# Second attention of a two-layer block: value products in two column halves with their sums from a block of ones, absorbed queries in pairs of heads, the row of maxima carried by transfers

## What is computed

```python
q_hk  = (hidden_q @ Wq.T).reshape(Bv, Sv, H, K)            # H = 16, K = 128
q_big = apply_rope(einsum('bshk,hkq->bshq', q_hk, w_kc_q))  # 192 columns per head
kv_r  = apply_rope(kv_c)                                    # 1444 x 64
q_r   = einsum('bshq,hqr->bhsr', q_big, W_qr)
k_r   = einsum('bld,hdr->bhlr', kv_r, W_kr)
scores = einsum('bhsr,bhlr->bhsl', q_r, k_r)
attn  = softmax(scores, axis=-1)
ctx_c = einsum('bhsl,bld->bhsd', attn, kv_r)                # values are kv_r itself
ctx_lat = einsum('bhsd,hkd->bhsk', ctx_c, w_kc_kv)
out   = ctx_lat.reshape(...) @ Wo.T
```

## Time and profile before

| | |
|---|---|
| median of 3 runs | 3939.77 us |
| the profiled execution: its time, its span | 3932.55 us, 3930.8 us |
| PE busy | 3538.9 us, 90% of the span |
| DVE, ACT, POOL busy | 2027.9, 1375.3, 814.5 us |
| granted TensorE clock, mean | 0.94 of full |
| second attention, first wide product to last scores | about 945 to 3634 us |
| value products (L1352) | 3072 records, 1156.9 us |
| score products (L1340, L1341) | 3072 records, 630.5 and 538.3 us |

### The profile page before, as it was taken

How to read it: one execution, slowest core, us unless ns; L and a number is a source line. 1 busy time by engine, 2 the same in 40 slices (tenths; PEclk the granted TensorE clock), 3 DMA queues, 4 the chain that set the end, 5 groups by cost and what they waited for, 6 DMA issues and landing times. The chain is left out here.

```text
span 3930.8 us, 51787 instructions
## 1 busy us (share of the span) xinstructions
PE 3538.9 (90%) x16584; PEld 2434.5 (62%) x16592; DVE 2027.9 (52%) x3166; ACT 1375.3 (35%) x2778; POOL 814.5 (21%) x678
## 2 busy tenths in 40 slices
PE   6999799996999999999999999999999999999244
PEld 5777688884666566656656665665665666566122
DVE  5777644444543644544364454445445444542588
ACT  1333222221334243234324323433432343334256
POOL 0000122222210410311131131122014012210367
PEclk9999799997999999999999999999999999999666
DMA  3000100003000000000000000000000000000200
GB/s 94 0 0 0 41 0 0 0 11 86 7 18 15 9 17 17 13 8 19 17 5 17 18 12 14 15 17 3 17 19 11 15 13 19 3 16 9 76 11 23
DMA packets 65315, 69.40 MB, mean 18 GB/s; under 512 B 23464, under 2 KB 55560, under 8 KB 65026
## 3 DMA queue, kind: packets, MB, share of 16 engines
q1 hardware_dynamic: 65090, 66.55, 6.1%
HBM read 56.30 MB, written 10.04 MB: 17 GB/s over the span
## 5 line engine op out<-in xcount | busy, mean ns | idle before, releaser
L1352 PE MATMUL c_o_ps<-c_p,c_val 120*65 120x400 f32 (+1 forms) x3072 | 1156.9, 499 | 2.0 <-ACT c_onum L1198 2.0
L1084 DVE TENSOR_REDUCE c_mneg<-c_m_ps 128x1 fp32r<-128x1452 f32 (+1 forms) x448 | 746.7, 1667 | 748.7 <-PE c_m_ps L1263 748.0
L1221 ACT ACTIVATE c_p<-c_s_ps 120x400 f32<-120x400 f32 (+1 forms) x1536 | 691.2, 501 | 1041.2 <-PE c_s_ps L1341 1033.2
L1340 PE MATMUL c_s_ps<-c_q,c_k 128*120 128x400 f32 (+1 forms) x1536 | 630.5, 410 | 30.4 <-issue 28.1
L1352 PEld LDWEIGHTS c_o_ps<-c_p,c_val 120*65 120x65 f32 (+1 forms) x3072 | 420.6, 137 | 354.2 <-issue 315.6
L1341 PE MATMUL c_s_ps<-c_q,c_k 65*120 65x400 f32 (+1 forms) x1536 | 538.3, 350 | 0.0
L1263 PE MATMUL c_m_ps<-c_k,c_q 128*128 128x484 f32 (+1 forms) x1344 | 456.3, 448 | 19.0 <-DVE c_mneg L1084 9.8
L1263 PEld LDWEIGHTS c_m_ps<-c_k,c_q 128*128 128x128 f32 (+1 forms) x1344 | 231.0, 181 | 223.9 <-DVE c_mneg L1084 113.4
L1028 POOL TENSOR_TENSOR c_rot<-c_rc,c_rs 96x400 f32<-96x400 f32 x256 | 262.1, 1044 | 508.0 <-DVE c_rs L1113 265.1
L1340 PEld LDWEIGHTS c_s_ps<-c_q,c_k 128*120 128x120 f32 (+1 forms) x1536 | 285.7, 186 | 103.3 <-issue 76.5
L1341 PEld LDWEIGHTS c_s_ps<-c_q,c_k 65*120 65x120 f32 (+1 forms) x1536 | 286.9, 187 | 56.6 <-issue 39.1
(11 more groups left out here) (220 smaller groups left out, 4273.0 us busy)
## 6 DMA issues: line engine op xcount, KB each, us to landing
c_rdb<-l_denominators SPq DMA_DIRECT2D x64, 200.0 KB, 3.3
c_kv<-in_ctx SPq DMA_DIRECT2D x32, 360.0 KB
x_rows<-in_x SPq DMA_DIRECT2D x4, 800.0 KB
x_spill<-x_rows SPq DMA_DIRECT2D x1, 3200.0 KB
c_xa<-x_spill SPq DMA_DIRECT2D x8, 400.0 KB
c_xr<-x_spill SPq DMA_DIRECT2D x32, 100.0 KB
x_spill<-c_xr SPq DMA_DIRECT2D x32, 100.0 KB
d_rows<-x_spill SPq DMA_DIRECT2D x5, 640.0 KB, 11.3
```

Of the source, the lines that this page charges most:

```text
L1084: v.tensor_reduce(mneg[0:n, t, DL:DL + 1], m_ps[0:n, :, 0:4 * KP], AX.XY, ALU.max, negate=True).then_inc(mneg_ready, 1)
L1221: a.activation(p[0:k, u % 3, i * CQS // 2:(i + 1) * CQS // 2], s_ps[0:k, (2 * u + i) % 3, 0:CQS // 2], ACT.Exp).then_inc(exp_ready, 1)
L1340: pe.matmul(o, k1[j % 2][:, r * KP:r * KP + k], q1[:, j, cols], start=True, stop=False)
L1352: mm = pe.matmul(o_ps[0:VW, i, 0:CQS // 2], val[0:k, j % 2, r, :], p[0:k, u % 3, i * CQS // 2:(i + 1) * CQS // 2], start=(r == 0), stop=(r ...
```

## The change

1. **Values.** The 64 value rows are multiplied by the left and the right 400 columns into the two partition halves of one bank, `o_ps[i * 64 : (i + 1) * 64]`. The sums leave that product: a 120 x 32 block of ones is multiplied by four quarters of 200 columns, into partitions 0, 32, 64 and 96 of a bank `d_ps` of its own.
2. **Drain, normalisation.** One copy of 128 x 400 and one of 128 x 200 in place of two of 65 x 400; four short transfers spread the sums, two bring them back, and one multiplication of 128 x 400 takes the place of one of 64 x 800. The halves in `ct` are heads 0 to 3 and 4 to 7 of a chunk, so the order in which `cvo` is built changes too.
3. **Absorbed queries.** Two heads at a time, into the two partition halves of `d_ps`; the ring `rot` has four places; four copies and two subtractions follow per pair.
4. **Row of maxima.** `maxima_row` and its copy are gone. SP carries each of the seven columns `mneg[0:128, c, t]` to a stretch of row 64 of `q2`; the first scores of a chunk wait for all seven (`row_loaded`).
5. **Places.** In a group's head the keys are turned beside head 1 (was 3), the projection stands at head 5 (was 6), the maxima beside heads 4, 6, 7, 9, 10, 11, 12 (were 9 to 15); the projection beside tiles moves from tile 8 to 9. SP's order is rewritten.

```diff
-                        for i in range(2):
-                            mm = pe.matmul(o_ps[0:VW, i, 0:CQS // 2], val[0:k, j % 2, r, :], p[0:k, u % 3, i * CQS // 2:(i + 1) * CQS // 2],
+                        for i in range(2):
+                            pe.matmul(o_ps[i * DL:(i + 1) * DL, 0:HALFQ], val[0:k, j % 2, r, :], p[0:k, u % 3, i * HALFQ:(i + 1) * HALFQ],
+                                      start=(r == 0), stop=(r == NT - 1))
+                        for q in range(4):
+                            mm = pe.matmul(d_ps[q * 32:(q + 1) * 32, 0:QUART], ones[0:k, :], p[0:k, u % 3, q * QUART:(q + 1) * QUART],
                                            start=(r == 0), stop=(r == NT - 1))
...
+                def load_row(ch, j, c):
+
+                    sp.wait_ge(mneg_ready, PRIMED + (ch + 1) * NQT)
+                    sp.sem_inc(m.carrier, 1)
+                    for t in range(NQT):
+                        sp.dma_start(q2[DL:DL + 1, j, c * CQS + t * 128:c * CQS + t * 128 + QT[t]].bitcast(F32), mneg[0:QT[t], c, t:t + 1].bitcast(F32)).then_inc(row_loaded, 16)
...
                         if r == 0:
-                            pe.wait_ge(row_copied, PRIMED + (it * G + j) * CH + c + 1)
+                            pe.wait_ge(row_loaded, 16 * NQT * ((it * G + j) * CH + c + 1))
...
-                    sp.dma_start(den[:], onum[DL:DL + 1, :].rearrange("o (p f) -> o p f", p=S)).then_inc(den_loaded, 16)
+                    for i in range(4):
+                        sp.dma_start(den[i * S // 4:(i + 1) * S // 4, :], oden[32 * i:32 * i + 1, :].rearrange("o (p f) -> o p f", p=S // 4)).then_inc(den_loaded, 16)
...
-                    for i in range(2):
-                        a.activation(onum[:, i * CQS // 2:(i + 1) * CQS // 2], o_ps[0:DL + 1, i, 0:CQS // 2], ACT.Copy).then_inc(on_ready, 1)
+                    a.activation(onum[:], o_ps[:, 0:HALFQ], ACT.Copy).then_inc(on_ready, 1)
+                    a.activation(oden[:], d_ps[:, 0:QUART], ACT.Copy).then_inc(on_ready, 1)
...
+                    def absorbed(pair):
+                        n = gi * (H // 2) + pair
+                        pe.wait_ge(rot_ready, PRIMED + 4 * (n + 1))
+                        if pair >= 1:
+                            pe.wait_ge(q1_ready, PRIMED + 4 * n)
+                            pe.wait_ge(q2_ready, PRIMED + 2 * n)
...
+                        for a in range(2):
+                            for half in range(2):
+                                i = 2 * pair + half
+                                mm = pe.matmul(d_ps[half * DL:(half + 1) * DL, 0:T], m.mqk[:, a, HEADS[i], :], rot[:, i % 4, a, :], start=(a == 0), stop=(a == 1))
...
+        HEAD_MAX, HEAD_PROJECT = (4, 6, 7, 9, 10, 11, 12), 5
```

More of the change, by code:

```diff
@@ L897, in beside_tile @@
                 todo.append(("max", j, 1, LATER.index(at)))
-            if at == 8 and j > 0:
+            if at == 9 and j > 0:
                 todo.append(("project", j - 1))
-            if at == 9:
-                todo.append(("row", j, 1))
             if j + 1 < G:
@@ L906, in beside_tile @@
                     todo.append(("max", j + 1, 0, NEXT.index(at)))
-                if at == 22:
-                    todo.append(("row", j + 1, 0))
             elif at == 17:
@@ L949, in group @@
                         b = it * G + j
-                        spread_denominators(b * CH)
+                        if j > 0:
+                            spread_denominators(b * CH - 1)
+                        load_row(b * CH + 1, j, 1)
+                        if j > 0:
+                            store_rows(b - 1, j - 1, more)
                         if j == 0 and more:
@@ L1175, in _, with copy_queries @@
             def _(a):
-                def copy_queries(gi, i):
-                    n, h = gi * H + i, HEADS[i]
-                    cols = slice((h % 2) * CQS + (h // 2) * S, (h % 2) * CQS + (h // 2 + 1) * S)
-                    a.wait_ge(q_ps_ready, PRIMED + n + 1)
-                    for half in range(2):
-                        a.activation(q1[half * DL:(half + 1) * DL, :, cols], o_ps[0:DL, 1, 0:T].rearrange("p (b s) -> p b s", b=G),
-                                     ACT.Copy).then_inc(q1_ready, 1)
+                def copy_queries(gi, pair):
+                    a.wait_ge(q_ps_ready, PRIMED + gi * (H // 2) + pair + 1)
+                    a.sem_inc(m.carrier, 1)
+                    for i in range(2):
+                        for half in range(2):
+                            a.activation(q1[half * DL:(half + 1) * DL, :, head_cols(2 * pair + i)],
+                                         d_ps[i * DL:(i + 1) * DL, 0:T].rearrange("p (b s) -> p b s", b=G), ACT.Copy).then_inc(q1_ready, 1)
                 def copy_keys(b, j):
@@ L1226, in group @@
                                 copy_keys(it * G + at[0], at[0])
-                            if what == "row":
-                                copy_row((it * G + at[0]) * CH + at[1], *at)
                     drain((it * G + G) * CH - 1)
@@ L1364, in beside @@
                                 maxima(it * G + at[0], *at)
-                            if what == "row":
-                                maxima_row(it * G + at[0], at[1])
                             if what == "project":
@@ L1381, in group @@
                         values(*at)
-                pe.wait_ge(consts, PRIMED + 4)
+                pe.wait_ge(consts, PRIMED + 3)
                 turn_rows(0)
```

169 lines of the change are left out of this document (83 added, 86 removed).

## The result

| | time | against the kernel before |
|---|---|---|
| before | 3937.62 us, median of 4 runs | |
| after | 4108.35 us, median of 4 runs (4097.92 to 4114.00) | 1.0429, 95% interval 1.0407 to 1.0451 |
| predicted | 4049 us, 3930 to 4130 | 1.028 |

The change costs 4.3%, some 170 us where 109 were forecast. The time is inside the range, 60 us above the forecast: three terms were too low by 95 us together and one too high by 30. Working time grew far less than the span: PE is busy for 3577.6 us of 4108.2, where it was 3538.9 of 3930.8. The page after the change: PE's line of busy times, its groups of the tile, and the issue of the row's transfers.

What follows compares the result with a forecast made beforehand. PE's own stream in the second attention was taken as the bound. Tile +85, head -72, row products -40, row transfers +112 and clock +24 gave +109 on 3939.77 us: 4049 us, range 3930 to 4130.

Steps and rivals of the forecast that it cites:

- The tile: Second attention's tiles: cheaper values and ones but three shape switches make 2.19 us in place of 2.08, +85 us.
- The leftover of the head: 0.30 us of a head's 3.84 us not explained by its products, read as two shape switches of 0.15 us each.
- Vanishing switches: Rival: shape switches cost nothing in the steady tile, which takes 1.74 us; total 3713 us, chance 0.09.
- a free 64 to 32: Rival on the values-to-ones switch costing nothing: alone 3937 us, chance 0.1; with quick transfer issue 3838 us, chance 0.06.
- products one behind the other: Rival: products in separate partition parts do not run together in the tile; about 5340 us, chance 0.04.
- the first rival: Shape switches vanish in the steady tile, 1.74 us each; sum -227 us, so 3713 us, chance 0.09.
- The row's products removed: In tiles, 56 of 64 rows of maxima no longer cost PE 0.72 us each: -40 us.
- The row by transfers: At 24 example boundaries PE waits 4.65 us for seven SP transfers, 7.2 us from reduction to use: +112 us.
- The clock: Half clock on PE after waits for the row, 1 us taken for each of 24: +24 us.
- The head: Group heads: absorbed queries in pairs shorten the body by 10 us, the tail grows 1; eight groups, -72 us.
- a head bounded by DVE's waits for ACT: Sign that the forecast is wrong: the group's head would not shorten.
- At nothing: Drain, normalisation, the sums' four transfers and the context fetch were taken to cost no time.

Runs made afterwards that it cites:

- the run with 32 columns: Changed kernel with the value product made in four blocks of 32 weight columns in place of two of 64: 3995.90 us, ratio 1.0144.
- the stepwise transfers: Changed kernel with each of the row's seven transfers issued once its own step of maxima is reduced, not all behind the last: 3973.73 us, ratio 1.0101.
- the run with parts 3 and 5 alone: Kernel before with only absorbed queries in pairs and the new places in the head: 3920.59 us, ratio 0.9950.
- the steps spread: Head maxima moved to heads 4, 6, 8, 10, 12, 14, 15: 3794.27 us with 32-column values and stepwise transfers; 3848.12 us on kernel before with parts 3 and 5.
- the paired order: Scores of two tiles, then values of two, on the kernel with 32-column values and stepwise transfers: 3857.49 us; with spread head maxima and other tile places 3796.01 us.

## Why the prediction was right or wrong

- **The tile: right in kind, 0.03 us too low.** "Three switches, 0.45 us" gave 2.19 us and +85; the trace has 2.22 us, +0.145 x 768 = +111. Undoing parts 1 and 2 gives 104, twice; they make the heads 8 us shorter as well. The leftover of the head was the right row, and the value chosen for 64 to 32, equal to the other switches, was the right one of the two ends: the run with 32 columns took exactly this switch away and got 112 us back. The Trainium skill's rule that a change of tiling mode drains the engine (page "TensorEngine Tiling (Array Packing)", section "Key Properties") agrees with the 0.16 us per change here; its 2.38 for three column tiles ("TensorE: Matmul & The Clock Gate", "Measured speedup vs the span model") does not show here, where four take the time of one (0.34 us a turn).
- **Rivals on the tile.** Vanishing switches, a free 64 to 32 and products one behind the other are all ruled out by these rows. The sum of the first rival has a slip: with tiles of 1.74 us the slack before the need is 2.55 - 2 x 0.45 = 1.65 us and not 2.1, which makes it 3724 us and not 3713; nothing hangs on it.
- **The row's products removed, -40: right.** The tiles beside which they stood took 2.79 us and take 2.23, and at the end of an example the same.
- **The row by transfers, +112: right mechanism, issue mis-sized.** The slack of 2.55 us is in the trace to a hundredth. The time from reduction to use is 5.95 us and not 7.2: an issue is 0.6 us, between the bounds 0.29 and 1.0 but nearer to the middle than to L940's 0.79, and a transfer's start to use 2.08, as assumed. So 3.4 us a time, 82 us. Chunk 1 is covered, as said.
- **The clock, +24: too low by half.** I took 1 us per wait with 2.1 as the upper bound "in part of the cases". It is every one of the 24: beyond the wait itself the tiles at a boundary, from value start to value start, are together 1.6 to 3.1 us longer than with the stepwise transfers, 2.2 us on average, 54 us. So even the bound was too low, for a wait shorter than the one it came from (3.4 us, not 4.7). The 129 us that the stepwise transfers bring are these 82 + 54, within what the intervals leave.
- **The head, -72: the step that failed.** The working let PE's stream shrink by 11.5 us and kept 1.6 us of that back for the copies; it asked whether DVE's total work fits and not where DVE's reductions stand, so PE's wait for them was at nothing. The maxima had moved to heads 9 to 12, one after the other, exactly where PE had become quicker: between two steps without an absorbed pair PE has work for some 3 us (2062.93 to 2066.04), while DVE comes to the reduction only behind its products and a pair's subtractions and needs until 2068.59. The body has 5.8 us of idle time from that, and the tail grew by 1.7 us instead of 1; and I had taken the body from a window that was 1.2 us too long, so that "-10" promised 1.2 us that were not there. -33 in the heads of the changed kernel, -15 in those of the run with parts 3 and 5 alone. The number itself is near what the pairs can give: with the steps spread, a head takes 70.7 us in the median, 10 less than before. One of my own signs, "a head bounded by DVE's waits for ACT", named a part of it: at one of the two long waits DVE had waited 1.46 us for ACT, at the other not at all. What went away with the spreading is PE's wait for the reductions.
- **At nothing:** the drain, the normalisation and the sums' transfers show no new wait of PE; right. (One wait for the normalised product is in both kernels, 8.9 us before and 10.5 after.)
- **The sum.** +111 - 33 - 40 + 82 + 54 = +174, measured +169 (1.0429). The forecast's +109 was 26 short on the tile, 30 on the clock and 39 on the head, and 30 too high on the row. Its upper end had been built from "half clock at each wait" and "a third of the head's gain missing", which came, and more than that, and from slower issues, which did not. That the time lies inside is in part luck: with the row's wait as forecast, and the other terms as they came, it would have been some 30 us more, 4138 us.

## What to carry to other kernels

Where products of two shapes alternate on PE, count the changes of shape per turn and price them from a place that already has one; packing that halves the streaming time can lose to three switches, and can be saved by cutting the wider product into blocks of the other's shape. Small transfers that each depend on one step of a loop belong behind that step: issued as a burst behind the last they cost the sum of their issue times less the slack before the need, and a wait of PE of 3.4 us cost more than its length here, since a stretch at half clock came with it at all 24 places. When work leaves an engine that was the bound, look at where the other engine's instructions stand in that stretch, not only at how many there are, and move them apart.

## What the hardware showed that I had not expected

- Four f32 products of 400 columns in four blocks of 32 weight columns start within 0.02 us of each other and cost the time of one (0.335 us per record's turn).
- A change of shape costs 0.16 us on average and 0.10 to 0.24 by its place, most when the scores come last; there 0.10 us falls on the second product behind the change. That second delay does not belong to the shape: the scores' second product also starts 0.28 us behind the first, and not 0.18, behind the wait for the row (2602.02 to 2602.30 in the changed kernel) and in the paired order behind scores of its own shape (2236.78 to 2237.06).
- A wait of 3.4 us brought a stretch at half clock every time, but in 18 of 24 cases PE started at full clock and dropped 0.2 to 1.5 us later, while it was busy. After waits of 2.2 and 2.6 us in the head the bodies ran at a mean of 1.00 in some heads and 0.92 to 0.97 in others, with the same instructions; what decides this stays open.
- An SBUF to SBUF transfer of 128 single elements takes SP 0.47 us when issued by itself and 0.60 in a burst of seven, against 0.79 for one of 100 short rows from a single partition.
